# A vision block with a state-space mixer on one core: Softplus's rounding step as two ScalarE activations, and small steps of the main loop at other places

## The chip, the cores and the metric

The kernel runs on one NeuronCore of a Trainium2 chip. The core has five engines with a queue of their own each: TensorE (PE in the rows, its weight loads PEld), VectorE (DVE), ScalarE (ACT), GpSimd (POOL) and SyncE (SP), which here only issues DMAs. They meet through semaphores. The metric is the device time of one execution in microseconds (us), lower is better.

## The reference

64 images of 3x224x224 become 196 patches each; a class token stands ahead of them, so that an image is a sequence of L = 197 rows of 192 numbers. Cut to what matters:

```python
h = patches @ W.T + b; h = concat([cls_tok, h])            # (64, 197, 192)
# the mixer, on layernorm(h):
xz = x @ W_in; x_inner, z = split(xz)                      # 384 columns each
x_conv = silu(conv1d_4_taps(x_inner) + conv_b)
Bm, Cm = split(x_conv @ W_x)                               # 16 states each
delta = softplus(x_conv @ W_dt + b_dt)
A = -exp(A_log)
def step(h, t):                                            # 197 steps, 384 x 16 states
    h = exp(delta_t * A) * h + (delta_t * x_t) * B_t
    y_t = sum(h * C_t)
y = (ys + D * x_conv) * silu(z)
out = layernorm(y @ W_out) * gamma + beta
h = h + out
# then, on layernorm(h): a top-1 router over 8 experts with a capacity,
# gelu(x @ w1 + b1) @ w2 + b2, scaled by the router's probability
```

## The kernel before

The images go through the mixer in 32 pairs (N2 = 394 columns, the two images side by side). All engines run the same main loop, written out once for each pair as `body(i, r, on)`, and each pair is worked on in four bodies: pair i+2 is embedded and normalised at the front, pair i+1 gets its products and its Softplus, pair i is scanned, pair i-1 leaves through the output product, two normalisations and the store. A pair i is scanned in 12 units (3 blocks of 128 channels by 4 groups of 4 states). For one unit VectorE makes one product (`bx`, L1263) and two scans (`scan`, L1272, steps k = 2u and 2u+1). ScalarE makes the decay factors of a scan, two activations, straight into one of two PSUM buffers (`decays`, L654), so `decays(k)` may not begin before scan k-2 is done. GpSimd multiplies the scanned states by C (`times_c`, L478), and TensorE spreads B over the partitions for the next `bx` (`spread_b`, L941) and sums the states (`state_sum`, L952 and L956).

There are 24 steps k of VectorE and ScalarE, and 12 steps u of GpSimd and TensorE, in a body. The rest of the work stands at fixed steps, by lines such as

```python
                    if 1 in on and k == 15:
                        softplus_exp(i + 1)
```

and each engine goes through its list strictly in that order. On ScalarE that rest is: the three convolution products copied with their bias (L705), `silu_x` and `silu_z` (L730, L734), the B and C product (L710, L711), its middle part (L726), the delta products (L716 Relu and L717 Abs), the copies of z (L721) and of C (L696), the copies of the output product (L673), three normalisations (L661) and transposes (L689 to L691, L750, L751). Silu, Exp and Ln need a table load each when they follow another one (ACT_TABLE_LOAD rows).

Softplus(v) is made as relu(v) + ln(1 + exp(-|v|)), with the part that rounding 1 + e loses added back. ScalarE makes e = exp(-|v|) (`softplus_exp`, L738) and the logarithm (`softplus_ln`, L743); VectorE makes (e + 1) - 1 in one TENSOR_SCALAR (`softplus_t`, L1301); GpSimd adds e to relu(v) (L504), takes VectorE's result away (L510), adds the logarithm (`make_delta`, L515) and multiplies by x (`make_du`, L520). delta and du go to DRAM (L384) and come back repeated over the partitions (L393), which the scans of the next body need.

VectorE's rest is: `take_logits` (L1295), `take_y` (L1285, y times silu(z), three times), the statistics of three normalisations (L1246, L1251), `last_bc` (L1278), `softplus_t` and two `embed` (L1238). GpSimd's rest is `rstd` (L467 to L472) after each statistics, `rest_bc` (L484), `fill_rows` (L489), `apply_gamma` (L494) and `add_residual` (L500). Two PSUM banks (`kbank`) take all the small products of a body in turn; the table K_OF gives each of ten products its place, MADE and TAKEN the counts that its maker and its reader wait for, and each product on TensorE waits for the copy that empties its bank.

After the 32 pairs come the router, the sort into slots and 57 tiles of expert work, which the change does not touch.

## Time and profile before

| | us |
|---|---|
| median of 3 runs | 3364.38 (3360.92 to 3374.43) |
| the profiled execution's own time | 3366.22 |
| its span | 3364.2 |
| VectorE busy over the span | 2548.7 (76%) |
| TensorE busy over the span | 2541.2 (76%) |
| GpSimd busy over the span | 2403.7 (71%) |
| ScalarE busy over the span | 1908.0 (57%) |

The shares are means over two stages of different kinds: the main loop, from the first `bx` at 122.64 us to about 2470 us, and the router and the experts behind it. An engine's share of the loop is read from a window in the loop, not from this table. Times that are given below as "at +x" count from the start of the first `bx` of a body.

### The profile page before, as it was taken

To read this page: it belongs to the slowest core of one execution; us is meant where nothing else is said; L and a number is where in the kernel's file an instruction comes from. 1 tells how busy PE (TensorE), PEld (TensorE's weight loads), DVE (VectorE), ACT (ScalarE), POOL (GpSimd) and SP (SyncE) were. 2 spreads that over 40 slices of the span, in tenths; PEclk is the share of its full clock that TensorE was granted. 3 is DMA by queue.
4 is the path that set the end of the run, shared out by engine and by line. 5 is a ranking of instruction groups with operands and counts; after the bars stand their busy time and mean duration, and the time that the engine had idled before them with its cause. 6 is when DMAs were issued, how large, how long until landed. Compare 5 with 4: busy or idle time off the path is not lost.

```text
span 3364.2 us, 39121 instructions
## 1 busy us (share of the span) xinstructions
PE 2541.2 (76%) x12496; PEld 1551.2 (46%) x12496; DVE 2548.7 (76%) x2910; ACT 1908.0 (57%) x3720; POOL 2403.7 (71%) x1522
## 2 busy tenths in 40 slices
PE   5777888888788888878888887888531109989898
PEld 3444444444444444444444444444210107777777
DVE  1599999999999999999999999999957711212222
ACT  1567767777776777777677767767620003333332
POOL 0478887788888787888878878887745745655664
PEclk8898899899889998988999988899755559989999
DMA  2345553444555443455544444553300044555552
GB/s 88 87 97 118 127 121 95 94 94 102 119 126 121 96 94 94 101 121 126 120 97 94 94 100 119 125 123 84 80 15 0 0 70 159 181 172 175 180 184 98
DMA packets 185985, 361.06 MB, mean 107 GB/s; under 512 B 38891, under 2 KB 110131, under 8 KB 178402
## 3 DMA queue, kind: packets, MB, share of 16 engines
q1 hardware_dynamic: 165281, 329.75, 39.5%
q0 software_dynamic: 20544, 29.34, 2.8%
q8 instruction: 82, 1.34, 0.2%
q14 instruction: 78, 0.63, 0.1%
HBM read 294.03 MB, written 69.51 MB: 108 GB/s over the span
## 4 chain that ended last, share of the span: by engine, by line
DVE 32%; PE 28%; issue 17%; ACT 11%; POOL 6%; another core or an unknown queue 4%; DMA 2%; SPq 0%; DVEq 0%; POOLq 0%; ACTq 0%
DVE arena L1272 14%; DVE arena L1263 11%; PE banks L927 4%; PE banks L1174 4%; POOL slot_scratch L590 4%; PE banks L890 4%; PE banks L1158 2%; PE banks L918 2%; PE banks L956 2%; ACT banks L654 2%; ACT arena L661 1%; DVE arena L1246 1%; PE banks L1163 1%; DVE arena L1301 1%
## 5 line engine op out<-in xcount | busy, mean ns | idle before, releaser
L478 POOL TENSOR_TENSOR arena<-arena 128x1576 f32<-128x1576 f32 x384 | 1245.0, 3257 | 283.4 <-DVE arena L1272 283.4
L1272 DVE TENSOR_TENSOR_SCAN arena<-banks,arena 128x788 f32<-128x788 f32 x768 | 1359.8, 1789 | 57.5 <-ACT banks L654 19.2
L654 ACT ACTIVATE banks<-arena,neg_a 128x392 f32<-128x392 f32 x1536 | 842.8, 582 | 419.6 <-DVE arena L1272 412.2
L1263 DVE TENSOR_TENSOR arena<-arena,banks 128x1576 f32<-128x1576 f32 x384 | 681.2, 1774 | 26.9 <-DMA arena<-delta_du_scratch 17.6
L1500 DVE TENSOR_TENSOR arena<-banks,arena 128x384 f32<-128x384 f32 x57 | 31.8, 558 | 461.2 <-PE banks L1174 358.2
L956 PE MATMUL banks<-arena,gather_q 128*32 128x394 f32 x3072 | 378.4, 568 | 0.3 <-POOL arena L478 0.3
L890 PE MATMUL banks<-wtok,arena 128*99 128x192 f32 x1536 | 264.6, 330 | 49.1 <-ACT arena L721 44.3
L909 PE MATMUL banks<-arena,v_lo 128*128 128x394 f32 x768 | 288.1, 518 | 3.2 <-DVE logits L1295 1.7
L890 PEld LDWEIGHTS banks<-wtok,arena 128*99 128x99 f32 x1536 | 249.2, 167 | 81.3 <-ACT arena L721 65.6
L840 ACT ACTIVATE arena<-banks 128x256 f32<-128x256 f32 x57 | 22.0, 385 | 441.5 <-PE banks L1145 294.3
L1174 PE MATMUL banks<-arena 128*128 128x192 f32 x1368 | 253.2, 341 | 7.0 <-issue 6.0
L661 ACT ACTIVATE arena<-arena 99x192 f32<-99x192 f32 x384 | 178.9, 537 | 123.1 <-POOL arena L472 118.7
L1174 PEld LDWEIGHTS banks<-arena 128*128 128x128 f32 x1368 | 238.0, 201 | 12.6 <-issue 11.2
L619 POOL DMA_INDIRECT out_tokens<-arena x114 | 116.1, 1018 | 176.3 <-DVE arena L1505 151.6
L927 PE MATMUL banks<-arena,wdt 128*128 128x394 f32 x576 | 210.8, 511 | 5.7 <-ACT arena L730 4.9
L909 PEld LDWEIGHTS banks<-arena,v_lo 128*128 128x128 f32 x768 | 141.4, 194 | 151.5 <-issue 56.6
L900 PE MATMUL banks<-ident,arena 99*128 99x99 f32 x128 | 44.1, 370 | 215.5 <-ACT arena L691 126.3
L590 POOL DMA_INDIRECT slot_scratch<-arena x128 | 142.8, 1116 | 76.1 <-issue 38.7
L941 PE MATMUL banks<-arena,pick 128*128 128x394 bf16 x384 | 142.1, 370 | 72.5 <-DVE arena L1263 72.5
L1158 PE MATMUL banks<-arena 128*128 128x256 f32 x684 | 168.5, 397 | 14.7 <-ACT arena L842 12.5
L609 POOL DMA_INDIRECT arena<-rows_scratch,arena x114 | 117.0, 1026 | 71.9 <-DMA gate_scratch<-arena 37.4
L927 PEld LDWEIGHTS banks<-arena,wdt 128*128 128x128 f32 x576 | 105.3, 191 | 113.9 <-issue 29.2
(197 smaller groups left out, 4299.9 us busy)
## 6 DMA issues: line engine op xcount, KB each, us to landing
arena<-delta_du_scratch SPq DMA_DIRECT2D x384, 394.0 KB, 11.2
arena<-in_w_pack SPq DMA_DIRECT2D x57, 1155.0 KB
delta_du_scratch<-arena SPq DMA_DIRECT2D x96, 394.0 KB, 3.2
arena<-in_x SPq DMA_DIRECT2D x32, 1176.0 KB, 15.3
rows_scratch<-arena SPq DMA_DIRECT2D x32, 297.0 KB
rows_scratch<-arena SPq DMA_DIRECT2D x32, 294.0 KB
arena<-in_b SPq DMA_DIRECT2D x57, 96.0 KB
arena<-in_conv_w SPq DMA_DIRECT2D x1, 2304.0 KB, 8.6
```

What stands on the lines that cost most here:

```text
L478: pool.tensor_tensor(v[:, :, :], v[:, :, :], c_rep[r][:, u % NG].unsqueeze(1).to_broadcast([P, NQ, N2]), ALU.mult).then_inc(s_mulp, 1)
L590: pool.indirect_dma_start(out=slot_dram, out_offset=bass.IndirectOffsetOnAxis(ap=sidx[r][:, c:c + 1].bitcast(U32), axis=0), in_=sval[r][:, ...
L654: ins = act.activation(o, d, ACT.Exp, scale=neg_a[:, c:c + 1])
L661: ins = act.activation(dst(c), src(c), ACT.Identity, scale=rs[:, c:c + 1], bias=nb[:, c:c + 1])
L890: mm = pe.matmul(v[0:H0, f * DIM:(f + 1) * DIM], patches[:, c, b, f * HSTEP:f * HSTEP + H0], wtok[:, c, :], start=(c == 0), stop=(c == KP ...
L909: pe.matmul(v[:, 0:N2], v_lo[:, k, c], t_lo[:, :, k:k + L], start=(k == 0), stop=False)
L927: mm = pe.matmul(v[:, 0:N2], wdt[:, k, c], xz[r][:, k, :], start=(k == 0), stop=(k == MB - 1))
L956: mm = pe.matmul(ps_y[q * 32:(q + 1) * 32, 0:N2], gather_q[:, :], hb[u % BUFS][:, q, :], start=False, stop=(g == NG - 1), skip_group_check ...
L1158: pe.matmul(hidden_part(g, f), wp[g][:, f * P:(f + 1) * P], x[:, 0, :], start=(f not in (2, 3)), stop=False, skip_group_check=True)
L1174: mm = pe.matmul(ps_out[:, f * DIM:(f + 1) * DIM], hid[g % 2][:, c, f * P:(f + 1) * P], w2[:, c, :], start=(c == 0), stop=(c == KF - 1))
L1263: dve.tensor_tensor(hb[u % BUFS][:, :, :], rep[m][:, :, 1, :], ps_b[:, 0:N2].unsqueeze(1).to_broadcast([P, NQ, N2]), ALU.mult).then_inc(s_ ...
L1272: dve.tensor_tensor_scan(v, decay[k % 2], v, 0.0, ALU.mult, ALU.add).then_inc(s_scan, 1)
```

## The change

`softplus_t` on VectorE is gone. In its place stand `softplus_up` (delta = 1 + e) and `softplus_t` (delta = delta - 1) on ScalarE, both activations with Identity, with a new semaphore between them. Beside that, some 50 small steps of the four engines stand at other places of the body, and the bank table and its waits follow them.

```diff
-        K_OF = (0, 1, 2, 6, 5, 7, 8, 9, 14, 13)
+        K_OF = (0, 1, 2, 5, 6, 7, 8, 10, 16, 13)
...
 # GpSimd
-                    if 1 in on and u == 6:
+                    if 1 in on and u == 5:
                         rest_bc(i + 1, o)
-                    if -1 in on and u == 7:
-                        rstd(i - 1, 2)
-                    if 1 in on and u == 8:
-                        softplus_sum(i + 1)
-                    if 1 in on and u == 8:
-                        softplus_rest(i + 1)
-                    if 1 in on and u == 8:
-                        make_delta(i + 1)
                     if 1 in on and u == 8:
                         make_du(i + 1, o)
...
+                    if -1 in on and u == 4:
+                        rstd(i - 1, 2)
+                    if -1 in on and u == 5:
                         apply_gamma(i - 1)
...
+                    if 1 in on and u == 6:
+                        softplus_sum(i + 1)
+                    if 1 in on and u == 7:
+                        softplus_rest(i + 1)
+                    if 1 in on and u == 7:
+                        make_delta(i + 1)
...
 # ScalarE
+            def softplus_up(n):
+                act.wait_ge(s_spe, n + 1)
+                need(act, s_ddu, DDU * n)
+                act.activation(delta[:, :, :], spe[:, :, :], ACT.Identity, bias=1.0).then_inc(s_spu, 1)
+
+            def softplus_t(n):
+                act.wait_ge(s_spu, n + 1)
+                act.activation(delta[:, :, :], delta[:, :, :], ACT.Identity, bias=-1.0).then_inc(s_spt, 1)
...
+                    if 0 in on and k == 5:
+                        silu_z(i, r)
...
-                    if 0 in on and k == 9:
-                        silu_z(i, r)
                     if 1 in on and k == 9:
                         silu_x(i + 1, o)
...
+                    if -1 in on and k == 11:
+                        out_norm(i - 1)
...
-                    if -1 in on and k == 14:
-                        out_norm(i - 1)
-                    if 1 in on and k == 15:
                         softplus_exp(i + 1)
+                    if 1 in on and k == 14:
+                        softplus_up(i + 1)
+                    if 1 in on and k == 14:
+                        softplus_t(i + 1)
+                    if 1 in on and k == 16:
+                        softplus_ln(i + 1)
...
 # TensorE
-                    if -1 in on and u == 3:
+                    if -1 in on and u == 2:
                         if 1 in on:
-                            pe.wait_ge(s_gev, 10 * (i + 1) + 3)
+                            pe.wait_ge(s_gev, 10 * (i + 1) + 2)
                         else:
                             pe.wait_ge(s_lg, i - 2 + 1)
                         out_product(i - 1, r, 0)
...
 # VectorE
-            def softplus_t(n):
-                dve.wait_ge(s_spe, n + 1)
-                need(dve, s_ddu, DDU * n)
-                dve.tensor_scalar(delta[:, :, :], spe[:, :, :], 1.0, -1.0, ALU.add, ALU.add).then_inc(s_spt, 1)
...
-                    if -1 in on and k == 10:
+                    if -1 in on and k == 9:
                         out_stats(i - 1)
                     if 0 in on and k == 14:
                         take_y(i, r, 0)
+                    if 2 in on and k == 14:
+                        embed(i + 2, r, r, 0)
                     if 1 in on and k == 15:
                         last_bc(i + 1, o)
-                    if 1 in on and k == 15:
-                        softplus_t(i + 1)
-                    if 2 in on and k == 15:
-                        embed(i + 2, r, r, 0)
...
-                    if -1 in on and k == 20:
+                    if -1 in on and k == 19:
                         row_stats(i - 1, o)
-                    if 0 in on and k == 22:
+                    if 0 in on and k == 21:
                         take_y(i, r, 1)
```

Three places show what moves. First VectorE, around steps k = 14 to 16 of a body, before (L1272 is a scan, L1285 `take_y`, L1278 `last_bc`, L1301 `softplus_t`, L1238 `embed`, L1263 `bx`):

```order
L1272 SCALAR_TENSOR_TENSOR arena<-banks,arena 128x788
L1285 TENSOR_TENSOR arena<-arena,banks 128x394
L1272 SCALAR_TENSOR_TENSOR arena<-banks,arena 128x788
L1278 TENSOR_TENSOR arena<-arena 32x394
L1301 TENSOR_SCALAR arena<-arena 128x3x394
L1238 TENSOR_TENSOR arena<-banks,tok_bias 99x384
L1263 TENSOR_TENSOR arena<-arena,banks 128x1576
```

and the same place of the change (its lines are 13 further down: L1285 is a scan, L1298 `take_y`, L1251 `embed`, L1291 `last_bc`, L1276 `bx`):

```order
L1285 SCALAR_TENSOR_TENSOR arena<-banks,arena 128x788
L1298 TENSOR_TENSOR arena<-arena,banks 128x394
L1251 TENSOR_TENSOR arena<-banks,tok_bias 99x384
L1285 SCALAR_TENSOR_TENSOR arena<-banks,arena 128x788
L1291 TENSOR_TENSOR arena<-arena 32x394
L1276 TENSOR_TENSOR arena<-arena,banks 128x1576
```

The TENSOR_SCALAR is gone, and the first `embed` has moved one scan up; no VectorE instruction has been added.

Second ScalarE, steps k = 13 to 17, before (L716 and L717 the delta products, L654 the decays, L661 `out_norm`, L738 Exp, L721 a copy of z, L743 Ln):

```order
L716 ACTIVATE arena<-banks,bdt 128x394
L717 ACTIVATE arena<-banks,bdt 128x394
L654 ACTIVATE banks<-arena,neg_a 128x2x196 x2
L661 ACTIVATE arena<-arena 99x192 x4
L654 ACTIVATE banks<-arena,neg_a 128x2x196 x2
L738 ACTIVATE arena<-arena 128x1182
L654 ACTIVATE banks<-arena,neg_a 128x2x196 x4
L721 ACTIVATE arena<-banks 128x394
L743 ACT_TABLE_LOAD
L743 ACTIVATE arena<-arena 128x3x394
```

and of the change (L717 and L718 the delta products, L655 the decays, L739 Exp, L744 `softplus_up`, L748 `softplus_t`, L753 Ln):

```order
L717 ACTIVATE arena<-banks,bdt 128x394
L718 ACTIVATE arena<-banks,bdt 128x394
L739 ACTIVATE arena<-arena 128x1182
L655 ACTIVATE banks<-arena,neg_a 128x2x196 x2
L744 ACTIVATE arena<-arena 128x3x394
L748 ACTIVATE arena<-arena 128x3x394
L655 ACTIVATE banks<-arena,neg_a 128x2x196 x4
L753 ACT_TABLE_LOAD
L753 ACTIVATE arena<-arena 128x3x394
```

The two Identity activations are added with no table load of their own; `out_norm` has gone up to k = 11 and Exp up to k = 13.

Third ScalarE, steps k = 4 to 9, before (L705 the convolution's copies, L734 `silu_z`, L730 `silu_x`, L673 a copy of the output product):

```order
L705 ACTIVATE arena<-banks,cb 128x394
L654 ACTIVATE banks<-arena,neg_a 128x2x196 x2
L734 ACT_TABLE_LOAD
L734 ACTIVATE arena<-arena 128x1182
L730 ACTIVATE arena<-arena 128x1182
L673 ACTIVATE arena<-banks 99x384
L654 ACT_TABLE_LOAD
```

and of the change (L706 the convolution's copies, L735 `silu_z`):

```order
L706 ACTIVATE arena<-banks,cb 128x394
L735 ACT_TABLE_LOAD
L735 ACTIVATE arena<-arena 128x1182
L655 ACT_TABLE_LOAD
L655 ACTIVATE banks<-arena,neg_a 128x2x196 x4
L706 ACTIVATE arena<-banks,cb 128x394 x2
L655 ACTIVATE banks<-arena,neg_a 128x2x196 x4
L674 ACTIVATE arena<-banks 99x384
L731 ACT_TABLE_LOAD
L731 ACTIVATE arena<-arena 128x1182
```

The two Silus, which shared one pair of table loads, stand four steps apart with a pair each: two table loads more in a body.

## Rows read from the trace of the kernel before

**Rows 1.** Windows: length, each engine's busy time, granted clock, DMA share, GB/s.
```profile
500.00:600.00 100.00, 85.79 (x410) 46.25 (x409) 96.92 (x91) 74.12 (x135) 78.32 (x43) 0.93 0.38 89
1097.50:1121.50 24.00, 23.40 (x122) 14.02 (x114) 23.02 (x22) 21.57 (x37) 19.02 (x11) 1.00 0.00 1
```
**Rows 2.** Who VectorE waited for in the loop, 225 to 2390: us, times, longest.
```profile
DVE arena L1272 <- ACT banks L654: 19.0, 30, 1.2
DVE arena L1263 <- PE banks L941: 6.0, 6, 1.8
```
**Rows 3.** VectorE in order of time: start, us, line, what, idle before it.
```profile
1075.98 1.77 DVE L1263 TENSOR_TENSOR arena<-arena,banks 128x1576 f32<-128x1576 f32 x1
...
1105.64 1.80 DVE L1272 TENSOR_TENSOR_SCAN arena<-banks,arena 128x788 f32<-128x788 f32 x1 [0.57 <-ACT banks L654]
1107.35 1.11 DVE L1246 BATCH_NORM_STATS2 arena<-arena 99x6 f32<-99x192 f32 x4
1108.87 1.77 DVE L1272 TENSOR_TENSOR_SCAN arena<-banks,arena 128x788 f32<-128x788 f32 x1
1110.55 1.77 DVE L1263 TENSOR_TENSOR arena<-arena,banks 128x1576 f32<-128x1576 f32 x1
1115.83 1.77 DVE L1263 TENSOR_TENSOR arena<-arena,banks 128x1576 f32<-128x1576 f32 x1
1122.49 1.38 DVE L1301 TENSOR_SCALAR arena<-arena 128x1182 f32<-128x1182 f32 x1
1123.79 0.55 DVE L1238 TENSOR_TENSOR arena<-banks,tok_bias 99x384 f32<-99x384 f32 x1
...
1149.53 1.77 DVE L1263 TENSOR_TENSOR arena<-arena,banks 128x1576 f32<-128x1576 f32 x1
```
**Rows 4.** Line 1301: its duration's minimum, median and maximum in ns, first and last start.
```profile
L1301 DVE TENSOR_SCALAR arena<-arena x32: 1384/1384/1385, 97.1 to 2374.0; 128x1182 f32<-128x1182 f32 x32
```
**Rows 5.** ScalarE in order of time, in the same body.
```profile
1101.64 1.18 ACT L730 ACTIVATE arena<-arena 128x1182 f32<-128x1182 f32 x1
1102.72 0.47 ACT L673 ACTIVATE arena<-banks 99x384 f32<-99x384 f32 x1
1103.21 1.28 ACT L654 ACT_TABLE_LOAD   x1
1104.51 1.10 ACT L654 ACTIVATE banks<-arena,neg_a 128x392 f32<-128x392 f32 x2
...
1115.71 1.86 ACT L661 ACTIVATE arena<-arena 99x192 f32<-99x192 f32 x4
1117.47 1.09 ACT L654 ACTIVATE banks<-arena,neg_a 128x392 f32<-128x392 f32 x2
...
1118.50 1.17 ACT L738 ACTIVATE arena<-arena 128x1182 f32<-128x1182 f32 x1
1119.60 1.10 ACT L654 ACTIVATE banks<-arena,neg_a 128x392 f32<-128x392 f32 x2
```
**Rows 6.** VectorE in another body, 640 to 670.
```profile
646.35 1.80 DVE L1263 TENSOR_TENSOR arena<-arena,banks 128x1576 f32<-128x1576 f32 x1 [1.83 <-PE banks L941]
...
665.93 1.80 DVE L1272 TENSOR_TENSOR_SCAN arena<-banks,arena 128x788 f32<-128x788 f32 x1 [1.20 <-ACT banks L654]
```
**Rows 7.** The window at the start of that body, columns as in rows 1.
```profile
636.20:641.50 5.30, 5.30 (x26) 3.31 (x26) 5.20 (x4) 2.20 (x4) 5.30 (x3) 0.50 1.06 322
```
**Rows 8.** GpSimd in order of time, in the body of rows 3.
```profile
1129.29 2.56 POOL L520 TENSOR_TENSOR arena<-arena 128x1182 f32<-128x1182 f32 x1
...
1143.96 16.10 POOL L478 TENSOR_TENSOR arena<-arena 128x1576 f32<-128x1576 f32 x5
```
**Rows 9.** TensorE in the next body: the two output products.
```profile
1171.31 3.98 PE L967 MATMUL banks<-wout,arena 128*99 128x192 f32 x23
```
**Rows 10.** ScalarE in order of time, later in that body.
```profile
1108.36 0.50 ACT L710 ACTIVATE arena<-banks 128x394 f32<-128x394 f32 x1 [0.37 <-PE banks L918]
1111.98 0.59 ACT L716 ACTIVATE arena<-banks,bdt 128x394 f32<-128x394 f32 x1
```

More of the change, by code:

```diff
@@ L261, in build @@
         s_spt = sem("softplus_rounded")
+        s_spu = sem("softplus_one_more")
         s_spc = sem("softplus_rest")
@@ L757, in body @@
                         decays(i, k)
-                    if 0 in on and k == 0:
+                    if 0 in on and k == 1:
                         copy_c(i, r, o, 3)
```

119 lines of the change are left out of this document (58 added, 61 removed).

## The prediction

> **What bounds the kernel now.** I read the page's busy shares first, then windows of the loop, then who waits for whom, then one body of VectorE, ScalarE and GpSimd in order of time. The page gives VectorE and TensorE 76% each, which is a mean over a loop and a tail that have different limits. A window in the loop [rows 1] separates them: VectorE is busy 96.92 of 100 us, TensorE 85.79, GpSimd 78.32, ScalarE 74.12. VectorE hardly waits there [rows 2]: 19.0 us in 30 waits for ScalarE's decays (about one per body) and 6.0 us for TensorE's spread of B. So the time of the loop is VectorE's list, one instruction behind the other, and a body lasts from one first `bx` to the next, 1075.98 to 1149.53, 73.55 us [rows 3]. What a second engine does costs nothing as long as it is not late for VectorE.
>
> The second window of rows 1 shows the danger. It is the stretch at +21 to +45 of a body: ScalarE is busy 21.57 of 24 us there, 90%, against 74% over the loop. There the change puts its new work.
>
> **What leaves VectorE.** One TENSOR_SCALAR per pair. It lasts 1.38 us, but what counts is from its start to the next start: 1122.49 to 1123.79, 1.30 us [rows 3]. It is the same each time, 1384 ns in all 32 [rows 4]; the first, at 97.1, comes before the first `bx` at 122.64, where VectorE is idle for long anyway. So 31 x 1.30 = 40.3 us. Nothing is added to VectorE. Its other moved steps (logits, `take_y`, three statistics, `embed`) last what they lasted; they cost only if what they wait for is late.
>
> **The stall at k = 10.** VectorE waits 0.57 us for the decay of scan 10 [rows 3]: ScalarE does two Silus with their two table loads and a copy in one step. By rows 5 the Silu costs 1.08 us from start to start, a copy 0.49, a load 1.30. In the change `silu_z` is at k = 5, so step 9 has two copies, two loads and one Silu: 4.7 us where it had 5.2 behind the decay of scan 9, and `out_stats` (1.52 us [rows 3]) now stands ahead of the fifth `bx`, which gives the decay of scan 10 that much more time. This stall goes: 19.0 us in all [rows 2].
>
> Step 5 gets a copy, two loads and a Silu, 0.5 + 2 x 1.30 + 1.08 = 4.2 us. The decay of scan 5 starts when scan 3 ends and takes 1.03; the decay of scan 6 then ends 1.03 + 4.2 + 1.03 = 6.3 us after scan 3. Scan 6 starts one unit (5.28 us, from 1110.55 to 1115.83 [rows 3]), one `take_y` (0.5) and one `bx` (1.9) after that point, 7.6 us. It is covered by 1.3 us; without the cover it would cost what it is late.
>
> Here a rule speaks against the change. The rows put a switch at 1.30 us: the load starts at 1103.21, the decay behind it at 1104.51 [rows 5]. The Trainium skill, page "ScalarE: Activation LUTs", section "What ACT_TABLE_LOAD costs", says that every switch costs some 1380 ns of drain on top of the load's 1283. By that page the two new switches would take 5.3 us instead of 2.6. The trace has the page's load but not its drain, so I go by the trace; what the rule would do is the last rival.
>
> **The two Identities.** No row of before shows Identity on 128x1182 values. The nearest is the Exp of the same size, 1118.50 to 1119.60, 1.10 us from start to start [rows 5]. From below it is bounded by a pair of decays, which is 784 columns in 1.03 [rows 5], from above by three delta copies of 394 columns, 0.59 each, 1.77 [rows 10]. I take 1.10, and 0.1 for the second, which waits for the first: 2.3 us. The order shows no table load for them.
>
> Are they covered? I lay ScalarE's work of the change from the end of scan 7, which releases the decay of scan 9, to the end of the decay of scan 15. Each activation frees the engine about 0.1 us before its printed end (L730: 1.18 printed, 1.08 to the next start). Seven decay pairs at 1.03 make 7.2; two output copies 0.9; two loads 2.6; `silu_x` 1.1; the two B and C copies (0.50 each printed) 0.8; `out_norm` 1.76 (1115.71 to 1117.47); three delta pairs (0.59 printed) 2.9; the middle part, about one such copy, 0.5; Exp 1.1; the Identities 2.3. Sum 21.2 us [rows 5, 10]. VectorE's list over the same stretch: three units 15.8, `bx` and scan 14 3.6, `out_stats` 1.5, `take_y` and `embed` 0.9, together 21.8 us [rows 3]. So ScalarE arrives 0.6 us before it is needed, with no idle time on the way. Each wait on the way eats from these 0.6: `out_norm` waits for GpSimd's `rstd`, which now follows the statistics directly, and the B and C copy waits for TensorE. I allow 0.15 us per body for jitter, 31 x 0.15 = 5 us lost. With the upper bound for the Identities (2 x 0.67 more) it would be 0.7 us per body, 22 us; with the lower bound nothing.
>
> **GpSimd and the DMAs.** GpSimd's work is the same, only earlier. `make_du` ended at +55.9 (1129.29 + 2.56 [rows 8]). In the change its Exp comes two steps earlier, and I get about +52.5, so the store and the repeated load that the next body's first decay needs have some 3 us more before a body that is 2 us shorter. The `times_c` backlog, five in a row from 1143.96 [rows 8], starts earlier too. No cost, no gain.
>
> **TensorE.** At +0 to +27 TensorE runs at VectorE's pace: three convolutions and the output products. The change does the first output product (half of 3.98 us [rows 9]) before the spread of B for the fourth `bx` instead of behind it, so that this spread comes 2.0 us later; but the router's products ahead of it come earlier, as their transposes wait for a row normalisation one step earlier. I take nothing at full clock. In a few bodies the granted clock stays at 0.50, the 1.2 GHz level, for the first 5 us [rows 7], and there `bx` waits 1.83 us for TensorE and a scan then 1.20 instead of 0.57 [rows 6], 2.5 us together. Three bodies of 32 show it. They stay as they are.
>
> **The sum.** 40.3 + 19.0 - 4.7 = 54.6 us less. The profiled execution took 3366.2 (its span 3364.2), so 3311.6; the median of the runs shown, 3364.4, is 1.8 us lower, and so is my forecast: 3310 us. The prologue stays: there the logarithm was ready 4 us before GpSimd wanted it. The router and the experts are not touched.
>
> **The rivals.**
> - *ScalarE binds at k = 12 to 15.* The cover is 0.6 us by my own sum, and the waits on the way could be longer than jitter. If the chain is 1.0 us late per body, the gain is 59.3 - 31 = 28 us: 3336 us. For it: 90% busy in that stretch already. Against it: even with 90% busy, rows 2 name only the one stall at k = 10.
> - *Nothing is gained.* The moved steps of VectorE wait now, above all `out_stats`, which stands at k = 9, right behind the second output copy, and the `take_y` steps, one scan earlier than before. VectorE's queue is in order, so scans stand behind them. 1.9 us per body of such waits give the whole 59 us back: 3364 us. For it: the second output copy ends only 0.9 us before `out_stats` by the sum above. Against it: each of these steps has some cover by that sum, and all would have to fail.
> - *Slower: TensorE at 1.2 GHz through the convolutions.* The slow bodies cost 2.5 us each [rows 6], and the clock was already down when the body began [rows 7]. The change regroups the transposes and spreads that TensorE does at low load at the end of a body. If the clock is still down at +5 in every body, 29 more bodies lose 2.5 us, and the first output product ahead of the spread doubles its 2.0 us there, another 1 us: 29 x 3.5 - 55 = +47 us: 3411 us. From 16 slow bodies on it takes the whole gain. Against it: mean clock in the loop is 0.93 [rows 1].
> - *The drain.* If each switch took 1.38 us more than its rows show, step 5 would be 2.8 us longer and 1.5 us late, and the stretch of step 9, which has its two switches also in the trace of before, would be 2.8 - 0.6 = 2.2 us late. 31 x 3.7 = 115 us more than 3305: 3420 us. The 1.38 us are the drain of the Trainium skill's page "ScalarE: Activation LUTs", same section. The rows speak against it: behind the load the decay starts at once [rows 5].
>
> **How the numbers follow.** About what a measurement of this kernel can tell from no change is 0.5%, 17 us: faster is below 3347.6, slower above 3381.2. The forecast has 0.67; its own range is 3298 to 3325. ScalarE late has 0.13 and is still faster. Nothing gained has 0.11, TensorE's clock 0.07, the drain 0.02. So faster 0.80, same 0.11, slower 0.09. The range from 3297 (all of 59 us and TensorE's slow bodies gone as well) to 3345 takes in the first rival and the upper bound of the Identities, and leaves out the rest.
>
> **What would show it.** In the profile of the changed kernel I expect: the body from first `bx` to first `bx` at 71.3 to 71.5 us; two Identity groups of 32 with 1.17 to 1.19 us; six table loads per body of 1283 ns; VectorE's waits for ScalarE under 8 us in all; VectorE busy 97% of a window of the loop, ScalarE about 80%. I am wrong if VectorE waits for the decays of scans 12 to 15 by more than 0.3 us per body, if it waits ahead of `out_stats`, or if more than six bodies have a `bx` that waits over 1 us for TensorE.

## The result, and the profile after

The change made the kernel 0.4% slower, which lies within the 0.5% that I had called no change, though its interval leaves 1 out: 3384.27 us (median of 8 runs, 3379.97 to 3389.07) against 3370.28 (8 runs) of the kernel before on the same chip, ratio 1.0044 [1.0032, 1.0057]. I had forecast 3310 us, and the range ended at 3345. The profiled execution took 3381.15 us, its span is 3379.4. From the first `bx` to the last pair's first `bx` (31 bodies) the loop takes 2292.3 us, where it took 2277.3: the 15.0 us more are about the whole difference of the spans (15.2).

Line numbers of the change: L1276 `bx`, L1285 scan, L1291 `last_bc`, L1298 `take_y`, L655 decays, L505, L511, L516, L521 GpSimd's Softplus steps, L479 `times_c`. Two lines of the page after: the busy times, which answer to the table of before, and the scans (line engine op, tiles, count | busy us, mean ns | idle before). Below them is a window of the loop, which answers to the first of [rows 1].

```profile
PE 2615.5 (77%) x12496; PEld 1586.7 (47%) x12496; DVE 2571.7 (76%) x2878; ACT 2057.0 (61%) x3846; POOL 2407.1 (71%) x1522
...
L1285 DVE TENSOR_TENSOR_SCAN arena<-banks,arena 128x788 f32<-128x788 f32 x768 | 1345.8, 1787 | 41.0 <-DVE arena L1276 0.9
```
```profile
500.00:600.00 100.00, 88.75 (x423) 49.09 (x422) 96.85 (x90) 81.65 (x142) 78.16 (x44) 0.93 0.36 84
```

VectorE has lost 32 instructions of 1.38 us (44 us), yet it is busy 23 us longer. The line that grew, by 57 us in all, is `last_bc`. It is one small instruction, which stands at k = 15 in both kernels (duration min/median/max in ns), first before, then after:

```profile
L1278 DVE TENSOR_TENSOR arena<-arena x32: 566/751/776, 92.0 to 2373.2; 32x394 bf16<-32x394 f32 x32
```
```profile
L1291 DVE TENSOR_TENSOR arena<-arena x32: 1859/2544/2568, 96.0 to 2386.8; 32x394 bf16<-32x394 f32 x32
```

And who VectorE waits for, 225 to 2390 us, answering to [rows 2]:

```profile
DVE arena L1276 <- issue: 9.9, 22, 0.8
DVE arena L1298 <- PE banks L970: 8.0, 16, 0.6
DVE arena L1276 <- PE banks L955: 6.0, 13, 0.5
...
DVE arena L1285 <- ACT banks L655: 0.4, 1, 0.4
```

The 30 waits for the decays are gone, as forecast. New are waits at three places of a body, up to +24, together 23.9 us. For 14.0 us of them the profile names TensorE. For 9.9 us ("issue") it names nothing; that they are waits for TensorE too is my reading. In the body shown below, the spread of B for that `bx` ends at 434.40, 0.10 us before the `bx` starts.

**First cause: `last_bc` lasts 2.54 us instead of 0.57 to 0.76.** It is the one instruction of VectorE in the loop with both inputs in SBUF. Here it is before, on VectorE and then GpSimd, in the body of [rows 3]:

```profile
1121.70 0.76 DVE L1278 TENSOR_TENSOR arena<-arena 32x394 bf16<-32x394 f32 x1
```
```profile
1119.75 2.28 POOL L504 TENSOR_TENSOR arena<-arena 128x1182 f32<-128x1182 f32 x1 [0.50 <-ACT arena L738]
1124.02 2.56 POOL L510 TENSOR_TENSOR arena<-arena 128x1182 f32<-128x1182 f32 x1 [1.99 <-DVE arena L1301]
```

L504 ends at 1122.03, `last_bc` 0.43 us later, at 1122.46; then GpSimd stands idle for 1.99 us, since L510 waits for VectorE's TENSOR_SCALAR, which stands behind `last_bc`. In the change L511 waits for ScalarE instead, and nothing keeps GpSimd back. The same place after, VectorE and GpSimd:

```profile
307.66 1.80 DVE L1285 TENSOR_TENSOR_SCAN arena<-banks,arena 128x788 f32<-128x788 f32 x1
309.49 2.54 DVE L1291 TENSOR_TENSOR arena<-arena 32x394 bf16<-32x394 f32 x1
312.06 1.80 DVE L1276 TENSOR_TENSOR arena<-arena,banks 128x1576 f32<-128x1576 f32 x1
```
```profile
305.82 3.27 POOL L479 TENSOR_TENSOR arena<-arena 128x1576 f32<-128x1576 f32 x1
309.03 2.57 POOL L511 TENSOR_TENSOR arena<-arena 128x1182 f32<-128x1182 f32 x1
311.74 2.56 POOL L516 TENSOR_TENSOR arena<-arena 128x1182 f32<-128x1182 f32 x1
```

`last_bc` starts 0.46 us after L511 has, and ends at 312.03, again 0.43 us after GpSimd's instruction, which ends at 311.60. From its start to the next it takes 2.57 us, where it took 0.79: 1.78 x 31 = 55 us. (The printed ends of GpSimd's instructions are rough; the reading rests on the offset being the same in nearly every body of both kernels.)

**Second cause: TensorE's clock over the convolutions.** Here are windows of the first 12 us of three bodies of the change (columns as in [rows 1]), which last 75.25, 74.84 and 73.04 us. Then come the last 13 us of a body of before and the first 12 of the next, which lasts 73.20 us.

```profile
410.99:422.99 12.00, 12.00 (x48) 6.56 (x47) 11.29 (x9) 6.05 (x12) 8.17 (x4) 0.62 1.07 243
486.24:498.24 12.00, 12.00 (x48) 6.58 (x48) 11.37 (x9) 6.05 (x12) 8.18 (x4) 0.63 1.07 245
561.08:573.08 12.00, 11.25 (x50) 5.70 (x50) 11.79 (x9) 6.06 (x12) 8.19 (x4) 0.86 1.07 260
```
```profile
1136.53:1149.53 13.00, 6.63 (x30) 3.39 (x30) 12.65 (x16) 9.94 (x26) 10.89 (x9) 0.58 0.95 197
1149.53:1161.53 12.00, 12.00 (x62) 5.91 (x62) 11.79 (x9) 5.90 (x12) 11.71 (x5) 0.89 1.08 240
```

So the low clock at a body's end is not new. In before it falls at +60 to +65 in nearly every body, and is back within 2.6 us of the next body's start in all but four of 31 bodies (three of those have it back at +9.8 to +9.9, and last 76.1 to 76.6 us). In the change it falls at +57 to +60, comes back for some us, and falls again at the body's end or just behind it. At +5 it is down in 30 of 31 bodies. The length of a body follows from when the clock is back: at +5.7 to +5.9, 73.0 to 73.4 us; at +7.5 to +7.9, 73.8 to 74.2; at +8.7 to +9.1, 74.7 to 75.3 (all but the first two and the last body).

Where the clock is low there (0.62 is a mix of 0.50, the 1.2 GHz level, and 1.00), TensorE falls behind, and VectorE waits for it three times; in the first of these bodies:

```profile
422.23 1.80 DVE L1276 TENSOR_TENSOR arena<-arena,banks 128x1576 f32<-128x1576 f32 x1 [0.50 <-PE banks L955]
...
428.19 0.57 DVE L1298 TENSOR_TENSOR arena<-arena,banks 128x394 f32<-128x394 f32 x1 [0.57 <-PE banks L970]
...
434.50 1.79 DVE L1276 TENSOR_TENSOR arena<-arena,banks 128x1576 f32<-128x1576 f32 x1 [0.45 <-issue]
```

The 31 bodies sum to 28 us over 31 times the shortest common body, 73.03; in before to 8 us over 31 times 73.19. So: -40 (TENSOR_SCALAR) - 19 (stall) + 55 (`last_bc`) + 20 (TensorE) = +16 us, against 15.0 measured in the loop.

### The profile page after: what moved, and what is told of

Its sections match the earlier page's. It is cut to its first block, busy times and chain, and to the rows that moved or that the text cites. A ratio compares the mean times of both kernels' runs of the same rounds, so it can differ in the third digit from the quotient of the medians.

```text
span 3379.4 us, 39214 instructions
## 1 busy us (share of the span) xinstructions
PE 2615.5 (77%) x12496; PEld 1586.7 (47%) x12496; DVE 2571.7 (76%) x2878; ACT 2057.0 (61%) x3846; POOL 2407.1 (71%) x1522
## 4 chain that ended last, share of the span: by engine, by line
DVE 33%; PE 30%; issue 16%; ACT 9%; POOL 5%; another core or an unknown queue 3%; DMA 2%; SPq 0%; DVEq 0%; POOLq 0%; ACTq 0%
DVE arena L1285 13%; DVE arena L1276 11%; PE banks L923 9%; POOL slot_scratch L591 4%; PE banks L925 4%; PE banks L1187 3%; PE banks L970 3%; ACT banks L655 3%; ACT arena L662 3%; DVE arena L1259 2%; DVE arena L1291 2%; PE banks L1171 2%; PE banks L981 2%; PE banks L1176 1%
## 5 line engine op out<-in xcount | busy, mean ns | idle before, releaser
L479 POOL TENSOR_TENSOR arena<-arena 128x1576 f32<-128x1576 f32 x384 | 1246.2, 3256 | 251.1 <-DVE arena L1285 251.1
L1285 DVE TENSOR_TENSOR_SCAN arena<-banks,arena 128x788 f32<-128x788 f32 x768 | 1345.8, 1787 | 41.0 <-DVE arena L1276 0.9
L655 ACT ACTIVATE banks<-arena,neg_a 128x392 f32<-128x392 f32 x1536 | 838.0, 581 | 383.4 <-DVE arena L1285 374.5
L1276 DVE TENSOR_TENSOR arena<-arena,banks 128x1576 f32<-128x1576 f32 x384 | 682.5, 1777 | 34.5 <-DMA arena<-delta_du_scratch 17.2
L923 PE MATMUL banks<-arena,v_lo 128*128 128x394 f32 x768 | 336.1, 588 | 1.7 <-ACT arena L692 1.3
L854 ACT ACTIVATE arena<-banks 128x256 f32<-128x256 f32 x57 | 21.9, 384 | 440.2 <-PE banks L1158 261.9
L955 PE MATMUL banks<-arena,pick 128*128 128x394 bf16 x384 | 138.7, 361 | 193.0 <-DVE arena L1276 191.5
L904 PE MATMUL banks<-wtok,arena 128*99 128x192 f32 x1536 | 266.7, 331 | 5.4 <-DVE skip L1244 4.8
L904 PEld LDWEIGHTS banks<-wtok,arena 128*99 128x99 f32 x1536 | 246.2, 167 | 45.9 <-issue 44.3
L923 PEld LDWEIGHTS banks<-arena,v_lo 128*128 128x128 f32 x768 | 165.4, 227 | 188.5 <-issue 126.4
L468 POOL TENSOR_TENSOR arena<-arena,small 99x4 f32<-99x4 f32 x96 | 19.5, 203 | 280.9 <-DVE arena L1264 280.9
L941 PE MATMUL banks<-arena,wdt 128*128 128x394 f32 x576 | 204.4, 499 | 4.6 <-ACT arena L718 2.9
L591 POOL DMA_INDIRECT slot_scratch<-arena x128 | 150.7, 1177 | 76.1 <-issue 38.7
L948 PE MATMUL banks<-arena,wz_lo 128*128 128x394 f32 x192 | 110.6, 664 | 82.7 <-ACT arena L697 52.9
L955 PEld LDWEIGHTS banks<-arena,pick 128*128 128x128 bf16 x384 | 40.6, 106 | 283.2 <-DVE arena L1276 246.1
```

What stands on the lines that cost most here:

```text
L479: pool.tensor_tensor(v[:, :, :], v[:, :, :], c_rep[r][:, u % NG].unsqueeze(1).to_broadcast([P, NQ, N2]), ALU.mult).then_inc(s_mulp, 1)
L591: pool.indirect_dma_start(out=slot_dram, out_offset=bass.IndirectOffsetOnAxis(ap=sidx[r][:, c:c + 1].bitcast(U32), axis=0), in_=sval[r][:, ...
L655: ins = act.activation(o, d, ACT.Exp, scale=neg_a[:, c:c + 1])
L904: mm = pe.matmul(v[0:H0, f * DIM:(f + 1) * DIM], patches[:, c, b, f * HSTEP:f * HSTEP + H0], wtok[:, c, :], start=(c == 0), stop=(c == KP ...
L923: pe.matmul(v[:, 0:N2], v_lo[:, k, c], t_lo[:, :, k:k + L], start=(k == 0), stop=False)
L941: mm = pe.matmul(v[:, 0:N2], wdt[:, k, c], xz[r][:, k, :], start=(k == 0), stop=(k == MB - 1))
```

## The experiments

Each ratio is against the kernel before on the same chip, whose median was 3289 to 3296 us on four of the chips and 3384 on the one with a_fill, a_hand_fill and a_hand_y22_fill; only the ratios, and the lengths of bodies, compare across chips. The change itself, run again beside a_hand, gave 1.0042 [1.0028, 1.0057].

> The changed kernel itself, so that the experiments and it stand on one chip. 1.0044 times before, as measured.

### What `last_bc` waits for

**a_lbc13**: the change with `last_bc` two steps earlier.

```diff
-                    if 1 in on and k == 15:
+                    if 1 in on and k == 13:
                         last_bc(i + 1, o)
```

> The changed kernel with last_bc, the only VectorE instruction of the loop with both inputs in SBUF, at k = 13 instead of k = 15; nothing else moves. Theory 'held by GpSimd': last_bc lasts 2.54 us in the changed kernel because a GpSimd instruction that began before it must end first; it ended 0.43 us after that end in every body looked at. At k = 13 a GpSimd product (L479) has only 0.5 us left when it comes, so it lasts about 0.9 us, a body gets 1.6 us shorter, and the kernel some 50 us faster than the change: 3335 us. Rival 'the time is in the instruction or in its place behind embed': 2.5 us stay, 3384 us.

Ratio 1.0744 [1.0726, 1.0762]. The opposite of what I expected; bodies of 81.9 us. GpSimd and then VectorE:

```profile
967.98 3.26 POOL L479 TENSOR_TENSOR arena<-arena 128x1576 f32<-128x1576 f32 x1
971.20 2.27 POOL L505 TENSOR_TENSOR arena<-arena 128x1182 f32<-128x1182 f32 x1
973.44 3.23 POOL L479 TENSOR_TENSOR arena<-arena 128x1576 f32<-128x1576 f32 x1
976.63 2.54 POOL L511 TENSOR_TENSOR arena<-arena 128x1182 f32<-128x1182 f32 x1
```
```profile
970.83 8.77 DVE L1291 TENSOR_TENSOR arena<-arena 32x394 bf16<-32x394 f32 x1
```

Of the 8.9 us by which these bodies are longer, 6.2 are in `last_bc`; most of the rest is an `embed` that waits for its product on TensorE, 73.8 us in 29 times. `last_bc` does not wait for the instruction in flight alone. Each GpSimd instruction here starts 0.03 to 0.04 us before the printed end of the one ahead, so there is no gap; `last_bc` sits out four of them and ends at 979.60, 0.43 us after L511's end at 979.17, the first that is followed by a gap.

**b_lbc16**: the kernel before with `last_bc` one step later, the converse.

```diff
-                    if 1 in on and k == 15:
+                    if 1 in on and k == 16:
                         last_bc(i + 1, o)
```

> The kernel before with last_bc moved two steps down VectorE's list, behind the scan of k = 16, and nothing else. There GpSimd has L510, L515, L520 and the first two reciprocal-root steps back to back (1124.02 to 1131.8 in the trace of before) with gaps of at most 0.15 us; then it waits for the statistics that stand behind last_bc on VectorE. Theory that a VectorE instruction with both inputs in SBUF waits for a gap in GpSimd's queue: last_bc starts at about 1127.1, and is held until GpSimd runs dry at 1131.85, so it lasts about 5.1 us instead of 0.75, 4.4 us x 31 = 136 us more, about 3425 us, ratio 1.04. Rival, it waits only for the instruction in flight (L515, to 1129.14): 2.5 us, 53 us more, ratio 1.016. Rival, the length of last_bc has nothing to do with GpSimd: 0.75 us, ratio within 0.5% of 1.

Ratio 1.0117 [1.0101, 1.0132]. The main number of my expectation (1.04) was wrong, and its miss shows how small a gap is enough. By itself this run fits the rival of the one instruction in flight as well; only a_lbc13 tells the two apart. (The diff puts it one step k down; the expectation's "two steps" counts `softplus_t` and `embed`.)

```profile
993.46 2.41 POOL L515 TENSOR_TENSOR arena<-arena 128x1182 f32<-128x1182 f32 x1 [0.15 <-ACT arena L743]
996.01 2.69 POOL L520 TENSOR_TENSOR arena<-arena 128x1182 f32<-128x1182 f32 x1
```
```profile
994.70 1.59 DVE L1278 TENSOR_TENSOR arena<-arena 32x394 bf16<-32x394 f32 x1
```

L515 ends at 995.87, `last_bc` at 996.29, 0.42 us after. Between L515 and L520 there are 0.14 us, and this gap, which I had taken for none, is enough.

**b_lbc13**: the kernel before with `last_bc` at k = 13.

```diff
-                    if 1 in on and k == 15:
+                    if 1 in on and k == 13:
                         last_bc(i + 1, o)
```

> The kernel before with last_bc at k = 13 instead of k = 15, nothing else. In the trace of before a GpSimd product runs from 1115.99 to 1119.25 there and VectorE comes at about 1117.7. Theory 'held by GpSimd': last_bc ends at about 1119.7 and lasts 2.0 us instead of 0.76, 1.2 us more per body, 37 us slower than before: 3407 us. Rival: no change, 3370 us.

Ratio 1.0096 [1.008, 1.0113], some 30 us slower. That is near the 37 us that I expected, but by luck: `last_bc` lasts 566 ns, since it meets GpSimd's short `rstd` steps, with gaps of up to 0.34 us between them. What the kernel loses, it loses elsewhere. In the loop `bx` waits 21.8 us for TensorE (6.0 in before), an `embed` 12.4 us for its product and the scans 23.9 us for the decays (19.0); ten bodies, which have the low clock at their start, last 76.2 to 76.6 us.

**a_hand**: the change, in which GpSimd's L511 also waits for `last_bc`.

```diff
                 pool.wait_ge(s_spt, n + 1)
+                pool.wait_ge(s_bc3, n + 1)
                 pool.tensor_tensor(spv[:, :, :], spv[:, :, :], delta[:, :, :], ALU.subtract).then_inc(s_spc, 1)
```

> The changed kernel with one wait more: GpSimd's softplus_rest (L511) also waits for last_bc. last_bc gets VectorE 8.77 us long at k = 13 and 0.57 us long where GpSimd stood waiting, so theory 'VectorE gets its second SBUF input only in a gap of GpSimd' says: GpSimd stands idle when last_bc comes, it lasts 0.57 instead of 2.54 us, a body loses 2.0 us as long as TensorE keeps up, and up to 60 us are gained over the change; with theory 'TensorE at 1.2 GHz through the convolutions' on top, bodies come out near 73 us as long as the clock is low, and only some 20 us of the 60 are seen. Rival 'the wait on the way costs as much as it gives': no gain.

Ratio 0.9849 [0.983, 0.9869], 3244.39 us: faster than both kernels. One more wait on GpSimd, which makes it stand idle for 1.15 us, gives VectorE 1.97 us per body. GpSimd, then VectorE:

```profile
1026.33 3.27 POOL L479 TENSOR_TENSOR arena<-arena 128x1576 f32<-128x1576 f32 x1
1030.75 2.56 POOL L512 TENSOR_TENSOR arena<-arena 128x1182 f32<-128x1182 f32 x1 [1.15 <-DVE arena L1292]
```
```profile
1030.01 0.57 DVE L1292 TENSOR_TENSOR arena<-arena 32x394 bf16<-32x394 f32 x1
```

It gains 61.7 us on the change, where 31 x 1.97 makes 61.1; I had left open that the low clock would hide all but 20 of them. In the traces the loop is 57.9 us shorter, for VectorE waits 28.0 us at the places where it waited 23.9 in the change. The first cause is shown. Neither half of the change makes it alone, as the next two runs show: `last_bc` is no longer than before where only the Identities are put in (b_swap), and where only the steps are moved (a_dve_t).

### What the Identities and the moved steps do alone

**b_swap**: the kernel before with the two Identities at k = 15 and no step moved.

```diff
 # ScalarE
+                    if 1 in on and k == 15:
+                        softplus_up(i + 1)
+                    if 1 in on and k == 15:
+                        softplus_t(i + 1)
 # VectorE
-                    if 1 in on and k == 15:
-                        softplus_t(i + 1)
```

> The kernel before with the swap alone: the two Identities on ScalarE behind Exp at k = 15, VectorE's step gone, no step moved. Theory 'the swap is worth its row, the moved steps lose': last_bc stays at 0.75 us, a body gets 1.3 us shorter, 40 us faster than before: 3330 us. Rival 'the Identities make ScalarE late': VectorE waits for decays after k = 15, 3370 us or more.

Ratio 1.0432 [1.0415, 1.045]. `last_bc` lasts 749 ns here; ScalarE is late, and through it a product of TensorE (waits of VectorE, 225 to 2390; L1252 is `embed`, L904 its product, L1277 `bx`, L955 the spread of B, L1286 a scan, L655 the decays):

```profile
DVE arena L1252 <- PE banks L904: 103.8, 28, 5.1
DVE arena L1277 <- PE banks L955: 49.2, 49, 1.9
DVE arena L1286 <- ACT banks L655: 32.0, 29, 1.2
```

TensorE's clock has a part in it too. The two bodies whose first 10 us have a clock of 0.94 and 0.98 last 75.8 us; 25 others have 0.50 to 0.52 there and last 78.3 to 78.9. So of 5.3 us over a body of before about half goes with the low clock. The moved steps are what makes room for the Identities. With them, the change has 0.4 us of waits for the decays and none at `embed`.

**a_dve_t**: the change with the TENSOR_SCALAR back on VectorE and no Identities.

```diff
 # ScalarE
-                    if 1 in on and k == 14:
-                        softplus_up(i + 1)
-                    if 1 in on and k == 14:
-                        softplus_t(i + 1)
 # VectorE
+                    if 1 in on and k == 15:
+                        softplus_t(i + 1)
```

> The changed kernel with the swap alone undone: (e + 1) - 1 on VectorE again at k = 15 behind last_bc, no Identities on ScalarE, all moved steps kept. Theory 'held by GpSimd': softplus_rest on GpSimd then waits for VectorE, so GpSimd is idle when last_bc comes; last_bc falls from 2.54 to about 0.7 us, the added step costs 1.30, and the kernel is some 17 us FASTER than the change, 3367 us. Rival 'the swap gives 1.30 us per body and something else takes it back': 40 us slower than the change, 3424 us.

Ratio 1.0097 [1.008, 1.0114]. `last_bc` is 566 ns as expected, since L510 waits for VectorE again. But the bodies are 75.06 us, 17 us slower than the change in all instead of 17 faster; the granted clock is 0.50 from +60 of nearly every body to +9 of the next, and VectorE waits for TensorE (L1284 is `take_y`, L956 the state sums, L1262 `bx`, L941 the spread of B):

```profile
DVE arena L1284 <- PE banks L956: 39.2, 58, 0.9
DVE arena L1262 <- issue: 13.4, 31, 0.8
DVE arena L1262 <- PE banks L941: 11.6, 27, 0.5
```

### What TensorE's clock does

**a_warm** and **a_hand_warm**: the change and a_hand, with the spread of B made four times for units 10, 11 and 0, and the router's products twice, to the same result.

```diff
-                pe.matmul(ps_b[:, 0:N2], pick[:, u % NG, :], bc3[r], start=True, stop=True).then_inc(s_bb, 1)
+                for _ in range(4 if u in (0, 10, 11) else 1):
+                    mm = pe.matmul(ps_b[:, 0:N2], pick[:, u % NG, :], bc3[r], start=True, stop=True)
+                mm.then_inc(s_bb, 1)
...
-                for c in range(4):
+                for c in (0, 1, 2, 3, 0, 1, 2, 3):
```

> The changed kernel with TensorE kept busy in its slack at the end of a body: the spreads of B for units 10, 11 and 0 are made four times over and the router's products twice, with the same result. Theory 'the low clock through the convolutions costs VectorE waits': granted clock 1.0 for most of +0 to +12, VectorE's waits for TensorE from 30 us to under 8 us, bodies at 73.04 us, 30 us faster than the change. Rival 'TensorE has too much work there': slower than the change.

> Both edits. If both theories hold and nothing else is late, the body is 73.04 - 1.97 = 71.1 us and the kernel some 90 us faster than the change, about 2.2% under before. If TensorE's work alone is too much, no faster than with the one wait.

Ratios 1.0026 [1.0017, 1.0036] and 0.9914 [0.9893, 0.9935]. a_warm is 7 us faster than the change, where I expected 30; a_hand_warm is 20 us slower than a_hand, and `take_y` waits 30.0 us for TensorE in its loop, 21.9 in a_hand's. The clock is higher, in the mean 0.83 over the first 10 us of a body of a_warm against 0.67 in the change. Yet the waits at the three places fall only from 23.9 to 16.0 us. In the bodies read, most of the extra work is done at 1.00 and part at 0.50; the likely reason for the small gain is that the second set of router's products stands ahead of the convolutions and takes time itself. That was not taken apart, so this pair leaves the second cause open.

**a_hand_y22**, **a_hand_out**, **a_hand_y22_out**: a_hand with the `take_y` of k = 21 back at k = 22, with the first output product back behind the state sums (u == 3 for u == 2), and both.

```diff
-                    if 0 in on and k == 21:
+                    if 0 in on and k == 22:
                         take_y(i, r, 1)
...
-                    if -1 in on and u == 2:
+                    if -1 in on and u == 3:
...
                         out_product(i - 1, r, 0)
```

> a_hand with take_y of the second block back at k = 22, where it stands before the change. In a_hand 24 of 31 bodies have VectorE wait 0.71 to 0.74 us for TensorE at this take_y (at +66), since the eight state sums ahead of it take 1.54 us at granted clock 0.50. One scan later (1.75 us) they are done. Theory: 35 waits, 26.5 us in all, of which some 18 stand there; bodies of 71.93 become 71.2, so 18 us less than a_hand, about 3226 us, ratio to before 0.980 to 0.982. Rival: the wait only moves to the next bx or to the state sums of the third block (they wait for take_y), and the time stays at 3244.

> a_hand with the first output product back behind the state sums of u = 3, where it stands before the change. This tells what its place ahead of the spread of B costs. In a_hand 8 or 9 bodies, those in which the granted clock is low at their start, lose 0.4 to 0.6 us at each of the bx at +11, the take_y at +17 and the bx at +23. Theory that the place matters (my 2.0 us doubled at the low clock): most of these waits go, 5 to 8 us less than a_hand, ratio 0.982 to 0.983. Rival: the low clock alone makes them, they stay and the time is that of a_hand, 0.985.

> Both of the above in one kernel. If they are independent the gains add: 71.2 us in nearly all bodies, 3220 us, ratio 0.978 to 0.981. If TensorE's clock is what both hang on, the regrouping may move the low stretch and one of the two gains is lost: 0.982 to 0.985.

Ratios 1.0018 [1.0009, 1.0027], 0.9866 [0.9851, 0.9881] and 0.9994 [0.9985, 1.0003]. The output product's place makes no gain. Taking away a wait of 0.73 us in 24 bodies cost 56 us: the waits for TensorE went from the end of a body into the next one's start. The third kernel shows how. Its bodies go 71.06, 74.47, 74.77, 73.24, and so on in turn. Windows of the first 10 us of these four, in this order:

```profile
484.57:494.57 10.00, 10.00 (x57) 5.08 (x57) 9.79 (x8) 4.73 (x9) 7.29 (x3) 0.88 1.07 270
555.63:565.63 10.00, 10.00 (x41) 5.42 (x41) 9.80 (x8) 4.73 (x9) 7.30 (x3) 0.50 1.06 269
630.10:640.10 10.00, 10.00 (x41) 5.44 (x41) 9.79 (x8) 4.73 (x9) 7.29 (x3) 0.50 1.06 276
704.87:714.87 10.00, 10.00 (x45) 5.54 (x45) 9.79 (x8) 4.73 (x9) 7.29 (x3) 0.63 1.07 267
```

The same instructions in the same order: with the clock at 0.88 over the convolutions a body lasts 71.06 us, with 0.63 73.24, with 0.50 74.47 and 74.77. Where a body is short, the next one begins cold. The fall comes behind TensorE's idle stretch (TensorE at that place, then windows of +52 to +56 and +58 to +70 of the first body):

```profile
539.65 0.34 PE L956 MATMUL banks<-arena,pick 128*128 128x394 bf16 x1 [3.14 <-DVE arena L1277]
```
```profile
536.57:540.57 4.00, 0.92 (x9) 0.25 (x9) 3.79 (x10) 1.29 (x3) 4.00 (x3) 1.00 0.30 121
542.57:554.57 12.00, 9.02 (x31) 4.51 (x32) 11.69 (x16) 11.07 (x30) 11.69 (x12) 0.50 0.88 181
```

**a_fill**, **a_hand_fill**, **a_hand_y22_fill**: the change, a_hand and a_hand_y22 with TensorE's idle stretches behind +51 filled by repeats to the same result.

```diff
-                pe.matmul(kbank(CS[g], o)[:, 0:N2], pick[:, NG + g, :], bc3[r], start=True, stop=True).then_inc(s_cb, 1)
+                for _ in range((1, 18, 8, 1)[g]):
+                    mm = pe.matmul(kbank(CS[g], o)[:, 0:N2], pick[:, NG + g, :], bc3[r], start=True, stop=True)
+                mm.then_inc(s_cb, 1)
...
+                for _ in range(2 if t == Z + 1 else 1):   # the last copy of z, both its products
```

> The same filling on the changed kernel itself, with VectorE's hold of 1.8 us per body left in. The best bodies of the change are 73.03 us, the mean is 74.1. Theory that the clock makes the difference: all bodies near 73.03, 31 x 1.07 = 33 us less than the change, ratio 0.994 (the change: 1.0042). Rival, order of the work: 1.004 or above.

> The same filling on a_hand. At full clock the eight state sums before the take_y at +66 take 0.87 instead of 1.54 us, so its wait of 0.73 us goes too, and bodies of 71.93 become 71.2 without moving take_y: 3222 us, ratio 0.977 to 0.981. If the clock falls all the same: 0.985 or worse.

> a_hand_y22 with TensorE's idle stretches behind +51 filled: the second spread of C is made 18 times, the third 8 times and the last copy of z twice, each into the same bank with the same result. In a_hand_y22 the granted clock falls at +54 to +58, after 3.1 us in which TensorE stands idle. Theory (the idle stretches make the clock fall, and the low clock alone makes the bodies of 73 to 74.6 us): the clock stays at 1.00 or falls later and is back before the body's end, bodies come to 71.0 to 71.2 us, which is what I had forecast for the change, 3220 us, ratio 0.975 to 0.980. Rival: the long bodies are not the clock's doing but the order of TensorE's work; then the ratio stays at 1.00. Rival: the clock falls in spite of it, at the transposes; ratio 0.99 to 1.00.

Ratios 1.0039 [1.0021, 1.0056], 0.9828 [0.9806, 0.985] and 1.0009 [0.9996, 1.0021]. The clock stays up where it fell, and falls later instead, in a_hand_y22_fill at about +70, behind the stretch of transposes; windows of +58 to +68 and +72 to +80 of one body:

```profile
543.19:553.19 10.00, 7.43 (x43) 3.29 (x42) 9.69 (x14) 6.87 (x16) 9.69 (x11) 1.00 0.79 224
557.19:565.19 8.00, 7.19 (x36) 3.82 (x36) 7.90 (x8) 4.65 (x12) 6.60 (x4) 0.50 1.03 229
```

It is then low over the convolutions all the same, and the bodies keep their length. a_fill is the same case: of the two falls at a body's end only the first is gone, and the loop takes 2292.0 us. In a_hand_fill, where it is back sooner in every other body, bodies of 71.07 and 72.04 us take turns. Its gain on a_hand is within the two intervals.

**a_hand_fill2**, **a_hand_y22_fill2**: the last idle stretches, from +62 to +70, filled too.

```diff
-                pe.matmul(ps_b[:, 0:N2], pick[:, u % NG, :], bc3[r], start=True, stop=True).then_inc(s_bb, 1)
+                for _ in range({11: 3, 0: 8}.get(u, 1)):   # 11: 9 in a_hand_y22_fill2
+                    mm = pe.matmul(ps_b[:, 0:N2], pick[:, u % NG, :], bc3[r], start=True, stop=True)
+                mm.then_inc(s_bb, 1)
```

> a_hand_fill with 3 and 8 spreads in the same places. In a_hand_fill bodies of 71.07 us alternate with bodies of 72.04, and the latter are those which begin with the clock at 0.50 up to +7. Theory: they become 71.07 too, 14 us less, ratio 0.979. Rival: the added spreads delay the state sums ahead of take_y, nothing gained, 0.983 or more.

> a_hand_y22_fill with the stretches of 2.0 us behind the last spread of B and of 1.3 us behind the next body's first one filled as well (9 and 8 spreads in place of one). Theory (the clock falls after TensorE's idle stretches, and the low clock over the convolutions makes the bodies of 74.4 us): the clock stays at 1.00 over the end of most bodies, these last 71.06 us, ratio 0.975 to 0.982. Rival: TensorE's order makes the long bodies, ratio stays at 1.00. Rival: the transposes alone are little enough for the clock to fall at +70 all the same, ratio 0.995 to 1.00.

Ratios 0.975 [0.9736, 0.9763] and 0.9755 [0.9742, 0.9768]: 3213 and 3216 us, 2.5% under the kernel before and nearly 3% under the change. Of a_hand_fill2, first the page's clock over the span (40 slices), then the first 10 us of two bodies, then all waits of VectorE from 225 to 2290:

```profile
PEclk9899999999999999999999999999965556999999
```
```profile
476.43:486.43 10.00, 9.50 (x52) 5.03 (x51) 9.79 (x8) 4.64 (x9) 7.35 (x3) 1.00 1.07 277
547.49:557.49 10.00, 10.00 (x60) 5.01 (x59) 9.79 (x8) 4.69 (x9) 7.33 (x3) 1.00 1.08 264
```
```profile
DVE arena L1292 <- DVE arena L1283: 0.9, 2, 0.5
DVE arena L1283 <- issue: 0.4, 2, 0.3
DVE arena L1271 <- issue: 0.3, 2, 0.2
```

Bodies are 71.05 to 71.1 us but for a few of 71.3 to 71.4. VectorE hardly waits, and here the place of `take_y`, worth 56 us without the filling, is worth nothing. So the second cause is the clock and not the order of TensorE's work. (In a_hand_fill2 the clock still dips behind about half of the bodies, mostly from +67 to +72, four times from +2 to +6 of the next. In a_hand_y22_fill2 it is at 1.00 from the second body to the last, and bodies of 71.3 to 71.4 us come there as well.) This is shown for a_hand and the kernels made from it. The change itself with all stretches filled was not run; that the 20 us in it are the clock's rests on the lengths of its bodies against their clock.

## Why the prediction was wrong

- *What leaves VectorE.* 1.30 us per body, right: the body of a_hand_fill2, 71.06, is 2.13 below before's 73.19, of which 2.06 are the 1.30, the stall's 0.57, and 0.19 by which `last_bc` is shorter.
- *"Its other moved steps last what they lasted."* **This step failed.** `last_bc` was mis-sized by 1.78 us a body, 55 us in all. I costed an instruction only by what it waits for, and not by what runs beside it. The row was there to be read: 566, 751 and 776 ns for one instruction of one size are a spread that wants a reason, where the TENSOR_SCALAR has 1384 in all 32 [rows 4].
- *The removed wait.* I counted TENSOR_SCALAR's time but not that GpSimd waited for it, and so stood idle exactly behind `last_bc`. With GpSimd's own steps moved up as well, nothing kept it back there. I listed no rival in which GpSimd holds VectorE. The Trainium skill, page "SBUF — State Buffer", section "Who interferes with whom", states that a VectorE instruction with two SBUF inputs contends with a GpSimd instruction that reads SBUF, and its section "Summary: rules for kernel authors" that the second to issue waits until the first has finished. The first part agrees with all traces here. The second doesn't: in a_lbc13 the wait went over four instructions.
- *The stall at k = 10.* Right, it is gone: 0.4 us in one wait instead of 19.0 in 30.
- *The Identities.* Right; ScalarE after, duration in ns. They need no table load: each body has the six loads of 1283 ns that I had expected.

```profile
L744 ACT ACTIVATE arena<-arena x32: 1172/1174/1190, 95.1 to 2381.5; 128x1182 f32<-128x1182 f32 x32
L748 ACT ACTIVATE arena<-arena x32: 1189/1190/1192, 96.4 to 2382.7; 128x1182 f32<-128x1182 f32 x32
```

- *ScalarE binds* and *the drain*. Neither; the cover held and the two new switches cost VectorE nothing. The 4.7 us of jitter didn't show.
- *"I take nothing at full clock. Three slow bodies stay."* **This step failed too**, by 20 us. At full clock it was right: in a_hand_fill2, which has the output product ahead of the spread, nothing waits for it. But the rival of TensorE at 1.2 GHz, to which I gave 0.07, is what happened: its condition, the clock still down at +5, held in 30 of 31 bodies. Its price of 3.5 us was too high for the change, where 20 bodies lose 0.8 to 2.2 us and the others next to nothing. The 3.4 and 3.7 us of a_hand_y22_out (71.06 against 74.47 and 74.77) are near it only by luck: there the output product stands behind the spread, and the 1 us that I had for its place cannot be in them. My argument against the rival was the loop's mean clock of 0.93, which says nothing about the 10 us on which it depends: the same window of the change has 0.93 too.
- *Nothing is gained*, the rival nearest to the time, had another mechanism: waits ahead of `out_stats` and `take_y` by their new places. Those at `take_y` exist, but for TensorE and only in cold bodies.
- *What would show it.* None of my signs of being wrong came up: one wait of 0.4 us for the decays in the whole loop, none ahead of `out_stats`, and no `bx` that waits over 1 us for TensorE (the longest is 0.8). VectorE is 97% busy and ScalarE 82%, as I had said. An instruction that is held counts as busy, so `last_bc` shows in none of these, and only the length of the body, 73.0 us or more where I expected 71.3 to 71.5, gave it away.

With both causes taken away the loop takes 2201.7 us, 75.6 less than before; I had forecast 54.6 less. Of the other 21 us, 5 are the jitter that didn't show, 6 are a `last_bc` shorter than in before, and 8 are before's own slow bodies.

What stays open: both kernels fall to the low level at the end of their bodies, but before has the clock back in time for the convolutions and the change has not. Why is shown only as far as that the falls follow TensorE's thin stretches, since filling them all ends the falls or gives the clock back in time. Which of the moved steps shifted the low stretch into the next body wasn't taken apart; and the fillings were sized by the idle times of the trace, without a search for the least that does.

## What to carry to other kernels

Before an instruction is moved or a wait removed, look at what the other engines do at that moment, and at whether the wait kept one of them quiet. An instruction whose duration has a spread may have such a neighbour. Where a kernel's busiest stretch follows a thin one on TensorE, read the granted clock over that stretch body by body: a shorter idle time somewhere else can cost more there than it gives.

## What the runs showed of the hardware

- The VectorE instruction with two SBUF inputs ended 0.42 to 0.43 us after the printed end of a GpSimd instruction in five kernels (before, after, a_lbc13, b_lbc16, b_swap), in all but one or two of their 32 bodies, and only of one that was followed by a gap. A gap of 0.14 us was enough. Over instructions that overlap by 0.03 to 0.04 us it starved, for 8.77 us against 0.57 when GpSimd is quiet.
- An added wait on GpSimd made the kernel 1.9% faster (a_hand against the change).
- 35 useless matmuls per pair took another 1% off (a_hand 0.9849, a_hand_fill2 0.975), because they kept TensorE's clock at the 2.4 GHz level over the work that followed.
- Bodies of one kernel, with the same instructions, lasted 71.06 to 74.87 us in a repeating order of four or five, by the clock with which each began.
